# Routed mixture of experts in three chunks, with results stored by tile and gathered by token

## The chip, the cores and the metric

The kernel runs on one core of one Trainium2 chip. The metric is the device time of one execution in microseconds. It was timed three times before the change: 2657.74, 2648.60 and 2647.09 us, median 2648.6 us.

## The reference, cut to what matters

The program is a stack of ten small layers over 8 sequences of 512 tokens with 128 channels (4096 tokens): `rwkv, attn0, moe0, alibi, attn0, moe0, light, moe1, diff, moe1`. The change touches the layer `moe1` alone, which is there twice, as the eighth layer and as the tenth and last. All it computes is this (x is layer-normalised before it, and the result is added to x):

```
xt = x.reshape(-1, embed_dim)                       # 4096 tokens x 128
logits = xt @ w_gate                                # 8 experts
top_logits, sel = jax.lax.top_k(logits, 2)
probs = jax.nn.softmax(top_logits, axis=-1)
h = silu(einsum('td,edh->eth', xt, w1)) * einsum('td,edh->eth', xt, w3)    # 256 wide
y = jnp.einsum('eth,ehd->etd', h, w2)
out = einsum('ktd,tk->td', y[sel.T, t_idx[None, :], :], probs)
```

The reference computes every expert for every token; the kernel computes only the two that each token has chosen.

## The kernel before, in words

A layer `moe1` is `routed_block`. Every engine has its own instruction stream, written by hand in program order, and the streams meet at semaphores. There is no scheduler: an instruction that waits holds up all that stands behind it on its engine.

**Preparation of a sequence** (`prepare`, in 14 steps): VectorE takes the statistics (`statistics`), GpSimd the power -0.5 of the variance (`token_scale`, L5034), VectorE the shift (`shifted`, L4876), ScalarE writes the normalised rows twice, once for each chosen expert (`tokens`, L4783); TensorE turns them and computes the 8 logits (`head_turned`, `gate`), VectorE picks the two largest (`chosen`), GpSimd computes an exponential (L230), VectorE the two weights (`weighted`), TensorE and VectorE the place of each row in its expert's region (`ranks`, `placed`). Then GpSimd issues 8 indirect DMAs (`sort`, L5043), each of which scatters 128 rows of 132 numbers (the token and its weight) to the tensor `sorted` in HBM. Step k of the sequence after comes 6 turns later. The rows have two buffers, so ScalarE's `tokens(j)` waits until the rows of sequence j-2 have landed in `sorted`.

**Tiles.** When all sequences of a chunk are sorted, `tabled` (L4929 to L4955, 14 operations of VectorE) makes a table: for each tile of 128 rows its expert's weights and its address. SP then writes a padding block behind each expert's rows (`pads`, 8 DMAs, L4620 and L4621), waits for them and for the sorted rows, and loads the tiles one after the other (`tile`, L4627 and L4628) into 10 slots of `xt`. A chunk of s sequences has 8s+7 tiles. One turn of the tile loop is on TensorE the product with w1 and w3 of tile i (`up`, L4716), the product with w2 of tile i-2 (`down`, L4732), the turning of tile i+2 (L4708) and of g of tile i-1 (L4724); on ScalarE silu and two copies from PSUM; on VectorE `result(i-2)` (L4969, PSUM to y) and `product_g(i)` (L4961, called g below). Into turns 0 to 31 of chunk 0 the preparation of the second chunk's sequences is woven.

**Way back.** Each row carries its destination (column `DEST`). GpSimd scatters each finished tile by it, one indirect DMA for each tile (`result`, L5048), to the tensor `results`, which is laid out by token. y has 4 slots; VectorE, before it fills a slot again, and SP, before it loads tile n, wait for such a scatter (`result_out`). SP later loads a sequence's results, two plain DMAs of 256 KB (`results`, L4634), and VectorE adds them to x (`added`, L4975 and L4977). The four sequences of chunk 0 are added within chunk 1, the four of chunk 1 behind the last tile.

A chunk's order on the engines is fixed by `turns(c)` (its tiles plus 2); `prepare(c + 1, i)` is called in turn i. In the eighth layer the first steps of the next layer (`opening`) stand in the last chunk; four of its operations are on GpSimd.

## Time and profile before

| | us |
|---|---|
| median of 3 runs | 2648.6 |
| profiled execution | 2655.23 |
| its span | 2653.5 |
| first routed layer: its start to the first g | 1540.0 to 1611.1 |
| its chunk 0 (39 tiles), first g to last g | 1611.1 to 1725.8 |
| its chunk 1 (39 tiles), first g to last g | 1749.2 to 1813.1 |
| its last addition ends | 1832.5 |
| second routed layer: first g to the last addition's end | 2430.9 to 2650.0 |

A profile gives each instruction's start and duration and, in square brackets, how long its engine stood idle before it and what ended that. Times are microseconds from the start of the span. Only one execution is profiled, and it took 6.6 us more than the median of the timed runs.

### The profile page before, as it was taken

Reading aid. Unit: us, or ns where it says so; the run is one execution under the profiler, and the core shown is the slowest. Engines: PE = TensorE matmul, PEld = TensorE weight load, DVE = VectorE, ACT = ScalarE, POOL = GpSimd, SP = SyncE. Lnnn points to the kernel's source line nnn. Section 1 sums busy time; section 2 is a strip of 40 time slices with the busy share of each in tenths; the row PEclk is TensorE's granted clock in tenths of the full one; section 3 lists DMA queues with packets and bytes.
Section 4 is the critical chain, followed back from the end, with each engine's and each line's share of the span. In section 5 each row is a group of like instructions: output and inputs, shape, how many; then the busy total and the mean of one; then the engine's idle time right before and its main releaser. Section 6 shows DMA issues by size and latency. Waiting matters only on the chain. (4 is left out here: it accounts for less than half of the span.)

```text
span 2653.5 us, 40505 instructions
## 1 busy us (share of the span) xinstructions
PE 2185.5 (82%) x11776; PEld 1305.5 (49%) x11776; DVE 1653.2 (62%) x4436; ACT 1286.1 (48%) x2268; POOL 1425.6 (54%) x1403
## 2 busy tenths in 40 slices
PE   4577997998779989979999945776999999964666
PEld 3344564666755556644444433444444444433444
DVE  6855775776667757756666643335787787743434
ACT  4633454332435533336666623443677677643334
POOL 5923754443347533436666654645676666525644
PEclk8778898999969989989999967887999999866788
DMA  1000111222011122210000032132000000021224
...
DMA packets 106957, 112.58 MB, mean 42 GB/s; under 512 B 21816, under 2 KB 86200, under 8 KB 106488
## 3 DMA queue, kind: packets, MB, share of 16 engines
...
## 5 line engine op out<-in xcount | busy, mean ns | idle before, releaser
L2332 DVE TENSOR_REDUCE l_diffneg_max<-psum 128x1 fp32r<-128x512 f32 x512 | 335.7, 685 | 101.7 <-PE psum L2070 92.9
L2247 ACT ACTIVATE l_diffweights<-psum 128x1024 f32<-128x1024 f32 x256 | 262.0, 1026 | 141.1 <-PE psum L2099 139.9
L2070 PE MATMUL psum<-l_diffkz,l_diffQ 128*128 128x512 f32 (+1 forms) x512 | 240.0, 488 | 2.7 <-DVE l_diffneg_max L2332 1.8
L5048 POOL DMA_INDIRECT results<-l_moe1y,l_moe1xt x156 | 149.6, 959 | 156.3 <-DVE l_moe1y L4969 136.3
L2871 ACT ACTIVATE l_lightswapped<-psum 32x512 f32<-32x512 f32 x304 | 179.0, 589 | 102.0 <-DVE l_lightturned L2963 98.6
L1597 DVE TENSOR_REDUCE l_attn0neg_max<-psum 128x1 fp32r<-128x512 f32 x256 | 167.2, 683 | 51.6 <-PE psum L1328 48.9
L1503 ACT ACTIVATE l_attn0weights<-psum 128x1024 f32<-128x1024 f32 x128 | 130.4, 1023 | 115.2 <-PE psum L1350 115.2
L1724 POOL TENSOR_TENSOR l_attn0half_sums<-l_attn0weights 128x2048 f32<-128x2048 f32 x30 | 137.2, 4572 | 86.2 <-ACT l_attn0weights L1503 86.2
L4296 ACT ACTIVATE l_moe0s<-psum 128x512 f32<-128x512 f32 x144 | 85.8, 596 | 198.7 <-PE psum L855 176.0
L4716 PE MATMUL psum<-l_moe1w,l_moe1zt 128*128 x312 | 178.4, 656 | 0.0
L4732 PEld LDWEIGHTS psum<-l_moe1w,l_moe1gt 128*128 128x128 f32 x624 | 92.5, 202 | 158.8 <-issue 158.6
L175 POOL TENSOR_TENSOR settled<-powers 128x1 f32<-128x1 f32 x97 | 24.4, 251 | 257.1 <-DVE l_alibimv L702 68.9
L223 POOL TENSOR_TENSOR l_moe0ex<-powers,l_moe0hot 128x32 f32<-128x32 f32 x14 | 76.5, 5468 | 154.3 <-DVE l_moe0hot L274 154.3
L4732 PE MATMUL psum<-l_moe1w,l_moe1gt 128*128 x624 | 104.7, 293 | 64.2 <-DVE l_moe1y L4969 40.7
L4217 PE MATMUL psum<-l_moe0g,l_moe0w_raw 128*128 128x512 f32 x288 | 148.3, 600 | 7.4 <-ACT l_moe0out_sb L4271 7.4
L2070 PEld LDWEIGHTS psum<-l_diffkz,l_diffQ 128*128 128x128 f32 (+1 forms) x512 | 97.4, 190 | 115.9 <-issue 68.4
L5043 POOL DMA_INDIRECT sorted<-l_moe1rows,l_moe1row_idx x128 | 124.0, 969 | 46.7 <-issue 35.8
L2485 POOL TENSOR_TENSOR l_difflow_rows<-l_diffwhole,l_diffmarks 128x512 fp32r<-128x512 f32 x63 | 65.5, 1040 | 144.3 <-ACT l_diffwhole L2231 141.7
L2113 PE MATMUL psum<-l_diffweights,x 128*32 128x512 f32 x1024 | 141.3, 625 | 0.0
L2099 PE MATMUL psum<-l_diffQ,l_diffkz 32*128 32x512 f32 (+1 forms) x512 | 131.8, 503 | 4.6 <-issue 3.2
L4961 DVE SCALAR_TENSOR_TENSOR l_moe1g<-l_moe1s,l_moe1xt,psum 128x256 f32<-128x256 f32 x156 | 73.6, 472 | 95.5 <-ACT l_moe1s L4805 95.5
L1328 PE MATMUL psum<-l_attn0K,l_attn0Q 96*128 96x512 f32 x256 | 123.2, 518 | 7.3 <-DVE x L1619 1.7
...
## 6 DMA issues: line engine op xcount, KB each, us to landing
...
l_moe1xt<-sorted SPq DMA_DIRECT2D x156, 66.0 KB, 1.8
l_attn0Q<-l_attn0q_hi SPq DMA_DIRECT2D x128, 64.0 KB
l_moe1yb<-results SPq DMA_DIRECT2D x32, 256.0 KB, 3.3
...
```

Source lines behind the costliest of these rows:

```text
L1597: nc.vector.tensor_reduce(neg_max[:, n % 2, st, hh:hh + 1], ps[:, bank_of(("max", n, b)), :], AXX, ALU.max, negate=True).then_inc(vec_max. ...
L1724: nc.gpsimd.tensor_tensor(halves[:, a, :, :], weights[:, 2 * a, :, :], weights[:, 2 * a + 1, :, :], ALU.add).then_inc(pool_sum.sem, pool_s ...
L2070: nc.tensor.matmul(ps[:, bank, :], Q[rows, n % 4, st * P:(st + 1) * P], kz[rows, n % 4, hh, :], start=True, stop=True).then_inc(pe_max.sem ...
L2099: ins = nc.tensor.matmul(ps[:, S[m % 2] + h, :], kz[rows, n % 4, hh, tt * P:(tt + 1) * P], Q[rows, n % 4, :], start=True, stop=True)
L2113: ins = nc.tensor.matmul(ps[strip(hh), O, :], V[:, j % 2, tt, g * PER_GROUP + hh, :], weights[:, tt, hh, :], start=(tt == 0), stop=(tt == ...
L2247: nc.scalar.activation(weights[:, tt, 2 * pair:2 * pair + 2, :], ps[:, S[m % 2]:S[m % 2] + 2, :], ACT.Exp, scale=SCALE).then_inc(act_exp.s ...
L2332: nc.vector.tensor_reduce(neg_max[:, n % 2, st, row:row + 1], ps[:, bank_of(("max", n, b)), :], AXX, ALU.max, negate=True).then_inc(vec_ma ...
L2871: copy = lambda to, frm: nc.scalar.activation(to, frm, ACT.Copy)
L4217: ins = nc.tensor.matmul(ps[:, OUT, :], weights_in.raw[:, c:c + P], g[:, n % G_RING, h, :], **ends)
L4716: nc.tensor.matmul(ps[:, H[n % 2], :], zt[:, n % 2, :], w[:, bass.ds(w_at, 4 * P)], start=True, stop=True).then_inc(pe_up.sem, pe_up.step( ...
L4732: ins = nc.tensor.matmul(ps[:, Y, 0:P], gt[:, n % 2, h * P:(h + 1) * P], w[:, bass.ds(w_at + (4 + h) * P, P)], start=h == 0, stop=h == 1)
L5048: p.indirect_dma_start(core.dram["results"], bass.IndirectOffsetOnAxis(ap=xt[:, n % SLOTS, R.DEST:R.DEST + 1].bitcast(U32), axis=0), y[:, ...
```

## The change: chunks, way back and tables

Three things are changed in `routed_block`, and some constants with them.

1. The 8 sequences go in three chunks of 3, 3 and 2, which have 31, 31 and 23 tiles (85 in place of 78 per layer). The constant operations at the start shrink: the padding block is kept once, the destinations are gone.
2. Finished tiles are no longer scattered by GpSimd. SP stores them in pairs by a plain DMA, in the order of the tiles (`pair`). VectorE works out in each chunk, in turn 4, for each token the two rows at which its results lie (`way_back`, 6 operations), and GpSimd gathers them with 8 indirect DMAs of 128 rows for each sequence (`gathered`). `GATHERED` and `ADDED` say in which (chunk, turn) the gathers are issued and the additions made; sequences 6 and 7 are gathered, and 5 to 7 added, behind the last tile. SP's tile load waits for g of the tile 10 before, no longer for a scatter.
3. `tabled(c)` follows at once on the placing of the chunk's last sequence, and its addresses of the padding blocks come first in it; SP writes the padding as soon as it has loaded the chunk before.

```diff
-    SEQS = (4, 4)
+    SEQS = (3, 3, 2)
+    GATHERED = {(1, 20): 0, (1, 27): 1, (2, 0): 2, (2, 6): 3, (2, 12): 4, (2, 18): 5}
+    ADDED = {(1, 30): 0, (2, 2): 1, (2, 8): 2, (2, 16): 3, (2, 22): 4}
```

On SP:

```diff
             def tile(c, t):
                 n = R.FIRST_TILE[c] + t
-                if n >= SLOTS:
-                    result_out(sp, n - SLOTS)
+                wait(sp, vec_g, n - SLOTS, "g")
...
-            def results(j):
-                wait(sp, vec_add, j - 2, "second")
-                for k in range(2):
-                    frm = core.dram["results"][k * NSEQ * T + j * T:k * NSEQ * T + (j + 1) * T, :]
-                    sp.dma_start(yb[:, j % 2, k, :, :], frm.rearrange("(q p) d -> p q d", p=P)).then_inc(y_loaded[j % 2], 16)
+            def pair(m):
...
+                wait(sp, vec_y, n + many - 1, "y")
+                sp.dma_start(core.dram["results"][c][t * P:(t + many) * P, :].rearrange("(t p) d -> p t d", p=P), y[:, m % PAIR_SLOTS, 0:many, :]
+                             ).then_inc(y_out[m % PAIR_SLOTS], 16)
...
             for c in range(R.CHUNKS):
+                n0 = R.FIRST_TILE[c]
                 pads(c)
+                if c:
+                    m = pairs_to(m, n0 - 8)
                 for j in range(max(last_of(c) - 1, 0), last_of(c) + 1):
                     rows_sorted(sp, j)
                 sp.wait_ge(padded[c], 16 * 8)
+                wait(sp, vec_table, c, "row")
                 for t in range(R.TILES[c]):
                     tile(c, t)
+                    if n0 + t >= 12:
+                        m = pairs_to(m, n0 + t - 12)
```

On VectorE:

```diff
             def tabled(c):
...
+                inc(v.tensor_copy(table[:, c, PAD_AT:PAD_AT + 8], run[:, :]), "pads")
                 inc(v.tensor_tensor(count[:, :], run[:, :], base[:, :], ALU.subtract), "count")
...
                 if due(c, k, 9) is not None:
                     placed(due(c, k, 9))
+                    if due(c, k, 9) == last_of(c):
+                        tabled(c)
...
             def result(n):
                 vec_y.start()
                 wait(d, pe_down, n, "down")
-                if n >= YS:
-                    result_out(d, n - YS)
+                m, half = place_of(n)
+                pair_out(d, m - PAIR_SLOTS)
...
                     prepare(c + 1, i)
+                    if i == WAY_BACK:
+                        way_back(c)
+                    if (c, i) in R.ADDED:
+                        added(R.ADDED[c, i])
```

On GpSimd:

```diff
-            def result(n):
-                wait(p, vec_y, n, "y")
-                p.indirect_dma_start(core.dram["results"], bass.IndirectOffsetOnAxis(ap=xt[:, n % SLOTS, R.DEST:R.DEST + 1].bitcast(U32), axis=0),
-                                     y[:, n % YS, :], None).then_inc(y_out[n % YS], 16)
+            def gathered(j):
+                c = chunk_of(j)
+                wait(p, vec_back, c, "back_idx")
+                if j == R.FIRST[c]:
+                    last = R.FIRST_PAIR[c] + R.PAIRS[c]
+                    for m in range(last - PAIR_SLOTS, last):
+                        pair_out(p, m)
+                wait(p, vec_add, j - 2, "second")
+                for k in range(2):
+                    for q in range(NQ):
+                        p.indirect_dma_start(yb[:, j % 2, k, q, :], None, core.dram["results"][c],
+                                             bass.IndirectOffsetOnAxis(ap=back_idx[:, j, k * NQ + q:k * NQ + q + 1], axis=0)
+                                             ).then_inc(y_loaded[j % 2], 16)
```

**GpSimd in chunk 0 of the first routed layer.** In a row before (`sorted` is a sort, `results` a scatter of a finished tile, `e` the exponential; x6 means six in a row):

```order
L5034 TENSOR_TENSOR l_moe1scale<-l_moe1var,powers 128x4
L5048 DMA results<-l_moe1y,l_moe1xt 10112x128 x6
L5034 TENSOR_TENSOR l_moe1scale<-l_moe1var,powers 128x4
L230 TENSOR_TENSOR l_moe1e<-powers,l_moe1p 128x4
L5048 DMA results<-l_moe1y,l_moe1xt 10112x128 x3
L5043 DMA sorted<-l_moe1rows,l_moe1row_idx 18304x132 x2
L5048 DMA results<-l_moe1y,l_moe1xt 10112x128
```

and now:

```order
L5072 TENSOR_TENSOR l_moe1scale<-l_moe1var,powers 128x4 x2
L230 TENSOR_TENSOR l_moe1e<-powers,l_moe1p 128x4
L5081 DMA sorted<-l_moe1rows,l_moe1row_idx 14208x132 x6
L5072 TENSOR_TENSOR l_moe1scale<-l_moe1var,powers 128x4
L230 TENSOR_TENSOR l_moe1e<-powers,l_moe1p 128x4
L5081 DMA sorted<-l_moe1rows,l_moe1row_idx 14208x132 x8
```

The scatters between the sorts are gone, so scale and exponential follow one another with no finished tile between them.

**GpSimd at the end of the same layer.** Before (`open_...` are the next layer's first steps):

```order
L5043 DMA sorted<-l_moe1rows,l_moe1row_idx 18304x132 x2
L5048 DMA results<-l_moe1y,l_moe1xt 10112x128 x42
L175 TENSOR_TENSOR settled<-powers 128x1
L453 TENSOR_SCALAR open_var<-open_mv 128x4
L457 TENSOR_TENSOR open_scale<-open_var,powers 128x4
L468 TENSOR_TENSOR open_z<-x,open_mv 128x512
L470 TENSOR_TENSOR open_z<-open_z,open_scale 128x512
L5048 DMA results<-l_moe1y,l_moe1xt 10112x128 x6
```

and now (`yb<-results` is a gather):

```order
L5081 DMA sorted<-l_moe1rows,l_moe1row_idx 14208x132 x10
L5094 DMA l_moe1yb<-results,l_moe1back_idx 128x128 x24
L175 TENSOR_TENSOR settled<-powers 128x1
L453 TENSOR_SCALAR open_var<-open_mv 128x4
L457 TENSOR_TENSOR open_scale<-open_var,powers 128x4
L468 TENSOR_TENSOR open_z<-x,open_mv 128x512
L470 TENSOR_TENSOR open_z<-open_z,open_scale 128x512
L5094 DMA l_moe1yb<-results,l_moe1back_idx 128x128 x40
```

Of the 64 gathers, 24 stand ahead of the next layer's steps and 40 behind them, the last 16 of which need the last tile's store.

**VectorE between two chunks.** Before, the table of chunk 1 stood behind the last two tiles' results (`y`), ahead of the next chunk's first two g:

```order
L4961 SCALAR_TENSOR_TENSOR l_moe1g<-l_moe1s,l_moe1xt,psum 128x256
L4969 COPY l_moe1y<-psum 128x128 x2
L4929 TENSOR_TENSOR l_moe1count<-l_moe1run,l_moe1base 128x8
L4931 TENSOR_SCALAR l_moe1whole<-l_moe1count 128x8
L4933 TENSOR_SCALAR l_moe1tiles_i<-l_moe1whole 128x8
```

and now it follows on `placed` of the last sequence, in turn 21 of chunk 0:

```order
L4937 TENSOR_REDUCE l_moe1row_at<-l_moe1picked 128x8
L4939 CAST l_moe1row_idx<-l_moe1row_at 128x8
L4940 TENSOR_TENSOR l_moe1run<-l_moe1run,psum 128x8
L4947 CAST l_moe1table<-l_moe1run 128x8
L4948 TENSOR_TENSOR l_moe1count<-l_moe1run,l_moe1base 128x8
L4950 TENSOR_SCALAR l_moe1whole<-l_moe1count 128x8
```

The 14 operations have moved from the gap between the chunks into the tile loop.

## Rows read from the trace of the kernel before

**Rows 1.** The page: span; busy us, share and instructions of each engine.

```profile
span 2653.5 us, 40505 instructions
...
PE 2185.5 (82%) x11776; PEld 1305.5 (49%) x11776; DVE 1653.2 (62%) x4436; ACT 1286.1 (48%) x2268; POOL 1425.6 (54%) x1403
```

**Rows 2.** Busy time by stretch: start:end, length, five engines, TensorE's clock, DMA share, GB/s.

```profile
core 0: us, PE busy (x) PEld busy (x) DVE busy (x) ACT busy (x) POOL busy (x), PEclk, DMA share, GB/s
1611.10:1726.30 115.20, 85.48 (x416) 57.17 (x414) 48.72 (x257) 50.98 (x149) 72.51 (x75) 0.86 0.20 59
1726.30:1749.20 22.90, 4.79 (x16) 2.86 (x17) 3.77 (x16) 1.32 (x5) 4.03 (x5) 0.57 0.18 52
1749.20:1813.60 64.40, 62.71 (x340) 41.64 (x338) 32.12 (x94) 38.22 (x119) 37.06 (x40) 0.99 0.36 105
1813.60:1832.50 18.90, 1.63 (x10) 1.21 (x10) 7.19 (x15) 0.38 (x1) 3.83 (x4) 0.62 0.44 128
2430.90:2545.30 114.40, 84.35 (x416) 57.07 (x414) 48.33 (x257) 50.77 (x149) 72.54 (x75) 0.86 0.20 60
2568.20:2630.80 62.60, 62.06 (x336) 41.11 (x334) 30.92 (x84) 37.05 (x113) 34.56 (x37) 0.99 0.44 127
```

**Rows 3.** Instructions by time, GpSimd, first routed layer's start (start, length, what, idle).

```profile
1577.84 0.96 POOL L5043 DMA_INDIRECT sorted<-l_moe1rows,l_moe1row_idx  x1 [0.97 <-DVE l_moe1run L4922]
...
1590.84 0.96 POOL L5043 DMA_INDIRECT sorted<-l_moe1rows,l_moe1row_idx  x1 [0.91 <-DVE l_moe1run L4922]
...
1599.67 0.96 POOL L5043 DMA_INDIRECT sorted<-l_moe1rows,l_moe1row_idx  x1 [0.30 <-issue]
```

**Rows 4.** The same stretch: the padding block's clearing, SP's pads and first tile loads.

```profile
1542.27 1.67 DVE L4850 MEMSET l_moe1spare<- 128x1935 f32 x1 [0.35 <-issue]
...
1594.87 8.50 SPq L4621 DMA_DIRECT2D sorted<-l_moe1spare  x8
1605.43 14.77 SPq L4628 DMA_DIRECT2D l_moe1xt<-sorted  x12
```

**Rows 5.** Chunk 0 by time: g of tiles 6 and 12, two waits of the preparation.

```profile
1623.97 0.47 DVE L4961 SCALAR_TENSOR_TENSOR l_moe1g<-l_moe1s,l_moe1xt,psum 128x256 f32<-128x256 f32 x1
...
1631.09 0.16 DVE L4876 SCALAR_TENSOR_TENSOR l_moe1shift<-l_moe1mv,l_moe1scale 128x4 f32<-128x4 f32 x1 [1.95 <-POOL l_moe1scale L5034]
...
1641.45 0.47 DVE L4961 SCALAR_TENSOR_TENSOR l_moe1g<-l_moe1s,l_moe1xt,psum 128x256 f32<-128x256 f32 x1
...
1656.36 3.18 ACT L4783 ACTIVATE l_moe1rows<-x,l_moe1shift,l_moe1scale 128x128 f32<-128x128 f32 x8 [8.55 <-DMA sorted<-l_moe1rows,l_moe1row_idx]
```

**Rows 6.** Between the chunks: table's first operation, SP's pads, first turned tile.

```profile
1728.80 0.16 DVE L4929 TENSOR_TENSOR l_moe1count<-l_moe1run,l_moe1base 128x8 f32<-128x8 f32 x1
...
1733.09 8.32 SPq L4621 DMA_DIRECT2D sorted<-l_moe1spare  x8
...
1745.30 0.48 PE L4708 MATMUL psum<-ident,l_moe1xt 128*128 128x128 f32 x1 [16.74 <-DMA l_moe1xt<-sorted]
```

**Rows 7.** DMA issues: count, KB of each, median us from issue to landing.

```profile
sorted<-l_moe1spare SPq DMA_DIRECT2D x32, 66.0 KB, 1.6
...
sorted<-l_moe1rows,l_moe1row_idx POOLq DMA_INDIRECT x128, 2.3
out<-x SPq DMA_DIRECT2D x8, 256.0 KB, 2.5
```

**Rows 8.** GpSimd's first and last operation for the next layer.

```profile
1807.04 0.21 POOL L175 TENSOR_TENSOR settled<-powers 128x1 f32<-128x1 f32 x1
...
1809.79 1.04 POOL L470 TENSOR_TENSOR open_z<-open_z,open_scale 128x512 f32<-128x512 f32 x1
```

**Rows 9.** Second layer: a scatter beside an addition, and the last addition.

```profile
2617.64 0.96 POOL L5048 DMA_INDIRECT results<-l_moe1y,l_moe1xt  x1 [0.68 <-DVE l_moe1y L4969]
...
2617.67 0.70 DVE L4975 TENSOR_TENSOR x<-x,l_moe1yb 128x512 f32<-128x512 f32 x1
...
2649.28 0.69 DVE L4977 TENSOR_TENSOR x<-x,l_moe1yb 128x512 f32<-128x512 f32 x1
```

More of the change, by code:

```diff
@@ L4518 @@
     WIDTH = P + 4
-    WEIGHT, DEST = P, P + 1
-    SPARE = 2 * NSEQ * T
+    WEIGHT = P
     COLS = 6 * P
+    PAIRS = [(many + 1) // 2 for many in TILES]
+    FIRST_PAIR = [0, *accumulate(PAIRS)][:CHUNKS]
+    GATHERED = {(1, 20): 0, (1, 27): 1, (2, 0): 2, (2, 6): 3, (2, 12): 4, (2, 18): 5}
+    ADDED = {(1, 30): 0, (2, 2): 1, (2, 8): 2, (2, 16): 3, (2, 22): 4}
+    OPENED = 2
     @staticmethod
@@ L4599, in rows_sorted, with place_of, pair_out @@
             engine.wait_ge(sorted_out[j % 2], 16 * 2 * NQ * (j // 2 + 1))
-        def result_out(engine, n):
-            engine.wait_ge(y_out[n % YS], 16 * (n // YS + 1))
+        def place_of(n):
+            c = max(c for c in range(R.CHUNKS) if R.FIRST_TILE[c] <= n)
+            pair, half = divmod(n - R.FIRST_TILE[c], 2)
+            return R.FIRST_PAIR[c] + pair, half
+        def pair_out(engine, m):
+            if m >= 0:
+                engine.wait_ge(y_out[m % PAIR_SLOTS], 16 * (m // PAIR_SLOTS + 1))
         @block.sync
@@ L4748, in _ @@
                 expert_of = lambda i: t.value_load(table[0:1, c, W_AT + i:W_AT + i + 1], min_val=0, max_val=7 * R.COLS)
-                wait(t, vec_table, c, "pads")
+                wait(t, vec_table, c, "row")
                 at_w = {0: expert_of(0)}
@@ L4954, in tabled, with way_back @@
                 inc(v.tensor_scalar(table[:, c, ROW_AT:ROW_AT + many], at_row[:, 0:many], float(8 * R.REGION + R.SPARES - 1), float(P), ALU.min, ALU.mult), "row")
-                inc(v.tensor_copy(table[:, c, PAD_AT:PAD_AT + 8], run[:, :]), "pads")
+            def way_back(c):
+                vec_back.start()
+                inc = lambda ins, key: ins.then_inc(vec_back.sem, vec_back.step(key))
+                wait_for = lambda key: d.wait_ge(vec_back.sem, vec_back.done(c, key))
+                many = R.SEQS[c] * 2 * NQ
+                mine = slice(R.FIRST[c], R.FIRST[c] + R.SEQS[c])
+                inc(v.tensor_tensor(first_tile[:, :], ends[:, :], tiles[:, :], ALU.subtract), "first_tile")
+                wait_for("first_tile")
+                inc(v.scalar_tensor_tensor(offset[:, :], first_tile[:, :], float(P), base[:, :], ALU.mult, ALU.subtract), "offset")
+                wait_for("offset")
+                inc(v.tensor_tensor(moved[:, 0:many, :], hots[:, mine, :, :].rearrange("p j k e -> p (j k) e"),
+                                    offset[:, :].unsqueeze(1).to_broadcast([P, many, 8]), ALU.mult), "moved")
+                wait_for("moved")
+                inc(v.reduce_sum(shifts[:, 0:many], moved[:, 0:many, :], AXX), "shifts")
+                wait_for("shifts")
+                inc(v.tensor_tensor(back[:, 0:many], shifts[:, 0:many], row_at[:, mine, :].rearrange("p j k -> p (j k)"), ALU.add), "back")
+                wait_for("back")
+                inc(v.tensor_copy(back_idx[:, mine, :].rearrange("p j k -> p (j k)"), back[:, 0:many]), "back_idx")
             def product_g(n):
@@ L5013, in _ @@
                     prepare(c + 1, k)
-            for j in range(R.FIRST[-1], NSEQ):
+            for j in range(len(R.ADDED), NSEQ):
                 added(j)
@@ L5063, in _ @@
             for c in range(R.CHUNKS):
-                n0 = R.FIRST_TILE[c]
                 for i in turns(c):
-                    if 0 <= i - 2 < R.TILES[c]:
-                        result(n0 + i - 2)
                     prepare(c + 1, i)
-                    if opening and c == R.CHUNKS - 1 and i == COMBINE + 2 + BETWEEN * R.SEQS[c - 1]:
-                        opening.scale(p)
-                        opening.tokens(p)
+                    if (c, i) in R.GATHERED:
+                        gathered(R.GATHERED[c, i])
+                        if opening and R.GATHERED[c, i] == R.OPENED:
+                            opening.scale(p)
+                            opening.tokens(p)
                 for k in spare_turns(c):
                     prepare(c + 1, k)
+            for j in range(len(R.GATHERED), NSEQ):
+                gathered(j)
 def product3(nc, out, x_hi, x_lo, w_hi, w_lo):
```

99 lines of the change are left out of this document (48 added, 51 removed).

## The prediction

> **What bounds the kernel now.** I read the busy time by stretch first, for the two routed layers alone, since nothing else is touched. The page shows a GpSimd that is busy 54% of the whole span [rows 1], which says nothing of these layers; the stretches do. In the first routed layer the tile loop of chunk 0 takes 114.7 us from the first g to the last (the stretch of 115.2 us less one g of 0.5), or 3.0 us for a tile; chunk 1, with as many tiles, takes 63.9 us; the second layer's chunk 1 takes 62.1 us, or 62.1 / 38 = 1.63 us for a tile, which I take as the loop's own pace [rows 2]. In chunk 1 TensorE is busy 62.7 of 64.4 us, in chunk 0 85 of 115 [rows 2]. So chunk 0 pays 114.7 - 38 x 1.63 = 52.7 us beyond the pace. Its four preparations cost part of that. The rest is GpSimd: it issues one indirect DMA every (1599.67 - 1590.84) / 7 = 1.26 us [rows 3], and its 75 instructions there [rows 2] are 67 DMAs (35 scatters, 32 sorts), 84.5 us at that pace, and 8 powers and exponentials of about 1 us each (72.5 busy us less 67 x 0.96); what it holds back is to be seen as VectorE's 1.95 us wait for a scale that stood behind a finished tile, and as ScalarE's 8.55 us wait for sorted rows that had not landed [rows 5].
>
> Between the chunks lie 1749.2 - 1725.8 = 23.4 us. The table starts only at 1728.80, SP's padding at 1733.09 takes 8.3 us, and the first tile is turned at 1745.30 [rows 6]. TensorE does 4.8 us of work in that stretch [rows 2]. Ahead of chunk 0 there is 71 us of preparation, in which each sequence costs 1590.84 - 1577.84 = 13.0 us [rows 3]. Behind chunk 1 there are 18.9 + 0.5 us of loads and additions [rows 2]. From the first g to the end of the last addition it is 221.4 us in the first layer and 2649.97 - 2430.9 = 219.1 us in the second [rows 2, 9].
>
> **Before chunk 0.** One sequence less is prepared: -13.0 us. The rest by what is late: the last sort is issued at 1599.67 and lands 2.3 us later, 1602.0 [rows 3, 7]; the padding is issued from 1594.87 to 1603.4 and lands 1.6 us after its last issue, and with the address's load the first tile is issued at 1605.43 [rows 4, 7]. With the pads' addresses first in the table, SP begins some 3.7 us earlier, so that the sorts become the last: with about 0.8 us for the address the tile goes out at 1602.8, -2.6 us. Clearing 7 blocks in place of 15 takes 0.8 us in place of 1.67 [rows 4]: -0.9. Sum -16.5 us in each layer. The lower bound is -13; for more than -16.5 a sequence would have to cost more than it does.
>
> **The tile loops.** 85 tiles in three chunks have 82 intervals in place of 76. A preparation without GpSimd's queue: the six turns from tile 6 to 12 hold one whole preparation, and took 1641.45 - 1623.97 = 17.5 us, 7.7 over the pace; the wait of 1.95 us for the scale lies in it [rows 5], and with scatters gone it goes. I take 5.5 us for each sequence, between 4 and 7.7.
> The table in the loop (14 operations, 1728.80 to about 1732.3, 3.5 us) finds some room in a turn, as VectorE is busy 30.9 / 38 = 0.8 of 1.63 us in the second layer's chunk 1 [rows 2], and some in the next: +2.3 us for each of two chunks, at most 3.5. The way back (6 small operations, estimated 1.5 us from the table's) fits beside the loop like an addition (2 x 0.7 us [rows 9]; the second layer's chunk 1 held four of them at 1.63 us a tile): 0, at most 1.5.
> Chunk 0, 31 tiles: 30 x 1.63 = 49.0, 3 preparations 16.5, table 2.3, TensorE's clock at the start 0.6 (an estimate; the granted clock was 0.86 over chunk 0 and 0.99 over chunk 1 [rows 2]), and tokens(5), which waits for the rows of sequence 3 (8 x 1.26 + 2.3 us plus scale and exponential of about 1 us each, against 5 turns that hold half a preparation) 1.5: 69.9 us. Chunk 1: 49.0 + 11.0 + 2.3 = 62.3, and 0.5 for the next layer's statistics in the first layer.
>
> **Between the chunks.** The pads are issued from turn 20 or 21 of the chunk before, last 8.3 us, and land 2 us later, in about turn 27; chunk 1's last sorts land 12.4 us after turn 21. So the tiles are there, and a boundary costs the drain and refill: 1728.8 - 1725.8 = 3.0, 1749.2 - 1745.3 = 3.9 and a little for the expert's address, 7.0 us in place of 23.4 [rows 2, 6], but twice.
>
> **From the last g of chunk 1 (time 0).** SP loads the next tiles at about the pads' pace, 8.32 / 8 = 1.04 us each [rows 6], with pair stores of an estimated 0.4 between them; the last pair of chunk 1 stands behind the 12th load, which waits for g of the second tile at 8.6 us. Issued at 10.1, landed at 12.1 (128 KB: between the 1.6 us of 66 KB and the 2.5 of 256 KB [rows 7]). GpSimd then issues the gathers of sequences 2 to 5, 32 x 1.26 = 40.4 us, to 52.5. The addition of 2, in turn 8 at 7 + 13 = 20 us, finds its rows landed only at 12.1 + 8.8 + 2.3 + 1.3 = 24.5: the loop stands 4.5 us. The last y is there at 7 + 22 x 1.63 + 4.5 + 2.8 = 50.2 us, its pair has landed at 52.6. Then 16 gathers: the last is issued 15 x 1.26 later, at 71.7, lands at 74.0, and the addition (1.4) ends at 75.5 us. In the first layer the next layer's four steps (1807.04 to 1810.8, 3.8 us [rows 8]) stand in GpSimd's queue: 79.3 us.
>
> **Sum.** First layer: 69.9 + 7.0 + 62.8 + 79.3 = 219.0 against 221.4. Second: 69.9 + 7.0 + 62.3 + 75.5 = 214.7 against 219.1. To this I add 4 us a layer for waits that such a sum misses (two handoffs at each of the boundaries, y's slots and SP's queue, each between 0 and the 1.95 us of [rows 5]; I take 1): 223.0 and 218.7. So the loops give back nearly nothing, and the gain is the start: -16.5 + 1.6 and -16.5 - 0.4, together -31.8 us. Profiled execution 2655.2 - 31.8 = 2623.4; the median lies 6.6 us lower than the profiled execution, so 2617 us.
>
> What the sum rests on and no row shows is the issue of a gather; the only row is that of the scatters, 1.26 us. Below it, at best, lies the 0.96 us of the instruction itself [rows 3]: 48 of them stand on the path of each layer, so -29 us for both. Upward I take 1.6 us as the bound of the range, +33 us.
>
> **A rule of the Trainium skill.** A scatter beside an addition, whose operands both lie in SBUF, took 0.96 us like every other [rows 9]. The page "SBUF — State Buffer", section "Who interferes with whom", says that a VectorE instruction with two SBUF inputs and a GpSimd instruction that reads SBUF block each other for the whole of the one that came first. The trace does not bear this out for scatters. If it came true for gathers, as a mechanism of this kernel: five additions of 2 x 0.7 us in each layer would hold GpSimd's chain, +7 us a layer, 2631 us in all.
>
> **The rivals.**
> 1. *The loops lose their waits more fully than I credit.* No missed handoffs (-8) and 4 us a preparation (-15 for ten): 2594 us; for it speaks that GpSimd has only 24 sorts in 31 turns.
> 2. *Chunk 0 stays coupled.* Sorts, scale, exponential and ScalarE's wait for landed rows also hold without scatters; chunk 0's 3.0 us a tile would make 90.6 us of it, +20.7 a layer, 2658 us, no change; half of it 2638. For it speaks the 8.55 us wait, which is for sorts [rows 5]; against it that in that stretch half of GpSimd's issues were scatters.
> 3. *The gathers become the bound, and it is slower than before.* Place: GpSimd from chunk 1's last store to the end. Each 0.1 us on a gather costs 48 x 0.1 x 2 = 9.6 us. From 1.60 us an issue the gain is gone, from 1.73 it is slower by over 0.5%; at 1.9 it would be 2678 us. For it: the gathers stand alone on the path at the end; against it: both directions describe 128 rows.
> 4. *SP comes late at the boundaries* (pads not ahead of the chunk's end): each boundary keeps its 23.4 us, +16.4 x 4, 2683 us. Against it: the pads need the placing of turn 21 (15 in chunk 1) alone.
> 5. *The port lock*, above: 2631 us.
>
> **How the numbers follow.** Forecast 0.60; rival 1 0.08; rival 2 0.14; rival 3 0.08; rival 4 0.05; rival 5 0.05. What a measurement of this kernel can tell from no change is about 0.5%, 13 us: faster is below 2635. The forecast, rival 1, rival 5 mostly (0.04) and a part of rival 2 (0.03) are faster: 0.75. The rest of rival 2 (0.11), 0.01 of rival 3, 0.02 of rival 4 and 0.01 of rival 5 are no change: 0.15. Slower is 0.10. Range 2598 to 2642: downward cheaper gathers and preparations, upward half of rival 2 and a gather of 1.5 us; the forecast's own range is 2603 to 2633.
>
> **What the new profile would show.** The first tile load of the first routed layer at about 1590 (the start); g of chunk 0 over about 70 us, with VectorE's wait for the scale short; 7 us from the last g of a chunk to the next g, twice; gathers at 1.26 us an issue, one after the other from about 12 us behind the last g of chunk 1 to the layer's end; one wait of VectorE of some 4 us ahead of the addition of sequence 2; 29 us (before 19.4) from the last g to the last addition. Wrong would be: chunk 0 over 80 us (rival 2), gathers over 1.5 us apart (3), pads behind the last y (4).

## The result, and the profile after

The changed kernel took 2616.95 us (median of 4 runs, 2610.84 to 2622.14) against 2653.17 us (median of 4, 2647.09 to 2657.81): a ratio of 0.9876, 95% interval 0.9849 to 0.9904. It is faster by 1.2%, and the forecast of 2617 us was met. That it was met to the microsecond is luck: the forecast was 2623.4 us for the profiled execution, which took 2619.28, and a median 6.6 us below it, where it lies 2.3 us below. How far the steps of the forecast were met is answered further down.

The page of the changed kernel, span and busy time:

```profile
span 2617.1 us, 41303 instructions
...
PE 2194.2 (84%) x11902; PEld 1310.5 (50%) x11902; DVE 1669.7 (64%) x4510; ACT 1297.8 (50%) x2310; POOL 1398.6 (53%) x1371
```

The busy time by stretch answers to [rows 2] (start:end, length, five engines, TensorE's granted clock as a share of 2.4 GHz, DMA share, GB/s). In order: chunk 0, the boundary, chunk 1, the boundary, chunk 2 and the way back of the first routed layer; then chunk 2 of the second.

```profile
core 0: us, PE busy (x) PEld busy (x) DVE busy (x) ACT busy (x) POOL busy (x), PEclk, DMA share, GB/s
1596.00:1673.90 77.90, 63.21 (x324) 43.30 (x322) 40.55 (x213) 39.00 (x115) 29.57 (x30) 0.91 0.28 76
1673.90:1680.10 6.20, 4.25 (x16) 2.52 (x17) 1.05 (x4) 1.73 (x6) 0.00 (x0) 0.87 0.33 89
1680.10:1742.40 62.30, 55.48 (x304) 37.07 (x302) 34.90 (x168) 35.34 (x106) 31.06 (x33) 0.99 0.35 94
1742.40:1750.60 8.20, 4.83 (x17) 2.87 (x17) 3.58 (x15) 1.74 (x6) 6.37 (x7) 0.76 0.52 137
1750.60:1788.30 37.70, 37.51 (x196) 24.54 (x194) 19.93 (x55) 22.07 (x69) 29.33 (x33) 0.96 0.41 114
1788.30:1819.00 30.70, 2.15 (x10) 1.62 (x10) 7.57 (x17) 0.77 (x2) 17.73 (x19) 0.55 0.17 49
...
2548.30:2584.20 35.90, 35.82 (x192) 23.40 (x190) 19.38 (x56) 20.80 (x65) 26.30 (x28) 0.99 0.51 139
```

GpSimd in chunk 0 is down from 75 instructions and 72.5 us to 30 and 29.6. The boundary of 22.9 us in [rows 2] has become one of 6.2 and one of 8.2. The last stretch, 18.9 us before, is 30.7 now, and in it GpSimd is the only engine with much to do.

SP in that layer answers to [rows 4, 6] (SPq: from the first issue to the last):

```profile
1578.81 8.63 SPq L4634 DMA_DIRECT2D sorted<-l_moe1spare  x8
1590.36 14.80 SPq L4640 DMA_DIRECT2D l_moe1xt<-sorted  x14
...
1655.72 8.43 SPq L4634 DMA_DIRECT2D sorted<-l_moe1spare  x8
...
1668.05 7.03 SPq L4640 DMA_DIRECT2D l_moe1xt<-sorted  x7
```

The pads of chunk 1 begin 18 us before the last g of chunk 0 (at 1673.90), and its first tile is requested 5.9 us before that g. GpSimd's gathers, the first of sequence 2 and those around the end of chunk 2:

```profile
1747.32 0.94 POOL L5094 DMA_INDIRECT l_moe1yb<-results,l_moe1back_idx  x1 [0.30 <-issue]
...
1787.98 0.94 POOL L5094 DMA_INDIRECT l_moe1yb<-results,l_moe1back_idx  x1 [0.30 <-issue]
1789.23 0.98 POOL L5094 DMA_INDIRECT l_moe1yb<-results,l_moe1back_idx  x1 [0.30 <-issue]
1790.52 0.94 POOL L5094 DMA_INDIRECT l_moe1yb<-results,l_moe1back_idx  x1 [0.30 <-issue]
1795.73 0.94 POOL L5094 DMA_INDIRECT l_moe1yb<-results,l_moe1back_idx  x1 [4.27 <-DMA results<-l_moe1y]
...
1815.16 0.94 POOL L5094 DMA_INDIRECT l_moe1yb<-results,l_moe1back_idx  x1 [0.30 <-issue]
```

and VectorE's additions beside and behind them, as [rows 9]:

```profile
1788.71 0.68 DVE L5012 TENSOR_TENSOR x<-x,l_moe1yb 128x512 f32<-128x512 f32 x1
...
1793.03 0.29 DVE L5006 COPY l_moe1y<-psum 128x128 f32<-128x128 f32 x1 [1.50 <-PE psum L4752]
...
1817.60 0.69 DVE L5012 TENSOR_TENSOR x<-x,l_moe1yb 128x512 f32<-128x512 f32 x1 [8.55 <-DMA l_moe1yb<-results,l_moe1back_idx]
1818.33 0.69 DVE L5014 TENSOR_TENSOR x<-x,l_moe1yb 128x512 f32<-128x512 f32 x1
```

The last y is copied at 1793.03, its pair is stored, and the first gather that needs it starts at 1795.73. The start of the sixteenth follows 19.4 us later; most are 1.25 us apart, the second 1.87. VectorE goes on 2.4 us after the last one's start, and its addition ends the layer at 1819.0. The issue of a gather costs what that of a scatter did.

The kernels side by side, in us, read from each trace as first routed layer / second; the four runs that come first below are not in the table. "Lead" runs from the layer's first VectorE instruction on the ranks' constants to the first g, a chunk from its first g to its last, a "gap" from there to the next g, "tail" from the last g to the last addition's end.

| kernel | ratio, 95% | lead | chunk 0 | gap | chunk 1 | gap | chunk 2 | tail | layer |
|---|---|---|---|---|---|---|---|---|---|
| before | 1 | 69.8/68.7 | 114.7/113.9 | 23.4/23.4 | 63.9/62.1 | | | 19.4/19.7 | 291.2/287.8 |
| changed | 0.9876 | 53.1/52.9 | 77.9/74.8 | 6.2/5.5 | 62.3/63.2 | 8.2/6.7 | 37.7/35.9 | 30.7/29.0 | 276.1/267.9 |
| early_again | 0.9894, 0.9857-0.993 | 67.2/66.7 | 115.9/115.1 | 9.4/7.7 | 64.4/62.2 | | | 19.8/20.1 | 276.7/271.8 |
| two_again | 0.9937, 0.9899-0.9975 | 65.9/65.9 | 96.9/101.2 | 5.9/5.5 | 64.5/62.1 | | | 48.5/48.4 | 281.6/283.1 |
| late_again | 1.001, 0.9969-1.0052 | 53.1/53.1 | 72.4/71.4 | 20.4/19.9 | 59.1/59.0 | 22.7/20.0 | 38.0/37.0 | 30.6/29.3 | 296.5/289.6 |
| rows3 | 0.9784, 0.9753-0.9814 | 51.1/50.2 | 68.3/70.1 | 5.5/6.2 | 63.1/62.0 | 8.1/6.4 | 38.1/36.4 | 30.1/28.9 | 264.2/260.2 |
| before_rows3 | 0.992, 0.9891-0.995 | 66.3/65.7 | 107.4/108.1 | 24.2/23.5 | 65.1/62.5 | | | 19.3/20.1 | 282.2/279.9 |
| early_rows3 | 0.9802, 0.9767-0.9836 | 64.2/63.8 | 111.0/112.5 | 6.1/5.5 | 63.5/61.8 | | | 19.5/20.3 | 264.3/263.8 |
| no_last_gathers | 0.9755, 0.9721-0.9788 | 53.3/53.0 | 76.8/73.2 | 5.5/5.5 | 61.6/61.6 | 8.1/6.6 | 38.0/36.3 | 21.6/20.4 | 264.9/256.5 |
| chunks_233 | 0.9976, 0.9953-0.9998 | 38.3/38.1 | 61.4/59.8 | 15.1/15.2 | 73.0/72.5 | 9.7/10.2 | 54.2/51.3 | 38.5/38.3 | 290.2/285.5 |

Of the 36.3 us between the two spans, 15.1 lie in the first routed layer and 19.9 in the second, 3.4 in the layer between them, which the change does not touch; against this, the stretch ahead of the first is 1.6 longer and the one behind the last addition 0.5. That untouched layer took between 517.8 and 530.2 us over the kernels of the table, so single traces are compared here by segments of the routed layers, and kernels by their ratios.

The four experiments that come first below ran in a set of executions in which the kernel before took 2706.49 us and the engines stood still inside the routed layers for nothing that the profile names; three of them were run again later ("again" in a name means that), `scatter_three` was not.

### The profile page after: what moved, and what is told of

It is laid out like the page before. It is cut to its first block and busy times, and to the rows that moved or that the text cites. A ratio compares the mean times of both kernels' runs of the same rounds, so it can differ in the third digit from the quotient of the medians.

```text
span 2617.1 us, 41303 instructions
## 1 busy us (share of the span) xinstructions
PE 2194.2 (84%) x11902; PEld 1310.5 (50%) x11902; DVE 1669.7 (64%) x4510; ACT 1297.8 (50%) x2310; POOL 1398.6 (53%) x1371
## 5 line engine op out<-in xcount | busy, mean ns | idle before, releaser
L2871 ACT ACTIVATE l_lightswapped<-psum 32x512 f32<-32x512 f32 x304 | 178.7, 588 | 100.6 <-DVE l_lightturned L2963 97.2
L1597 DVE TENSOR_REDUCE l_attn0neg_max<-psum 128x1 fp32r<-128x512 f32 x256 | 167.2, 683 | 50.6 <-PE psum L1328 47.8
L4736 PE MATMUL psum<-l_moe1w,l_moe1zt 128*128 x340 | 189.2, 640 | 0.0
L1724 POOL TENSOR_TENSOR l_attn0half_sums<-l_attn0weights 128x2048 f32<-128x2048 f32 x30 | 137.2, 4572 | 87.5 <-ACT l_attn0weights L1503 87.5
L4752 PEld LDWEIGHTS psum<-l_moe1w,l_moe1gt 128*128 128x128 f32 x680 | 98.3, 197 | 150.0 <-issue 150.0
L175 POOL TENSOR_TENSOR settled<-powers 128x1 f32<-128x1 f32 x97 | 24.2, 249 | 258.4 <-DVE l_alibimv L702 69.7
L4752 PE MATMUL psum<-l_moe1w,l_moe1gt 128*128 x680 | 112.4, 290 | 52.1 <-ACT l_moe1gt L4831 27.1
L2070 PEld LDWEIGHTS psum<-l_diffkz,l_diffQ 128*128 128x128 f32 (+1 forms) x512 | 97.0, 189 | 114.4 <-issue 66.7
L5094 POOL DMA_INDIRECT l_moe1yb<-results,l_moe1back_idx x128 | 122.6, 958 | 48.2 <-issue 39.4
L4371 DVE TENSOR_TENSOR l_moe0sc<-l_moe0s,l_moe0bcs 128x512 f32<-128x512 f32 x128 | 93.5, 730 | 56.0 <-ACT l_moe0s L4296 51.9
```

The costliest lines, as they stand in the source:

```text
L1597: nc.vector.tensor_reduce(neg_max[:, n % 2, st, hh:hh + 1], ps[:, bank_of(("max", n, b)), :], AXX, ALU.max, negate=True).then_inc(vec_max. ...
L1724: nc.gpsimd.tensor_tensor(halves[:, a, :, :], weights[:, 2 * a, :, :], weights[:, 2 * a + 1, :, :], ALU.add).then_inc(pool_sum.sem, pool_s ...
L2070: nc.tensor.matmul(ps[:, bank, :], Q[rows, n % 4, st * P:(st + 1) * P], kz[rows, n % 4, hh, :], start=True, stop=True).then_inc(pe_max.sem ...
L2871: copy = lambda to, frm: nc.scalar.activation(to, frm, ACT.Copy)
L4736: nc.tensor.matmul(ps[:, H[n % 2], :], zt[:, n % 2, :], w[:, bass.ds(w_at, 4 * P)], start=True, stop=True).then_inc(pe_up.sem, pe_up.step( ...
L4752: ins = nc.tensor.matmul(ps[:, Y, 0:P], gt[:, n % 2, h * P:(h + 1) * P], w[:, bass.ds(w_at + (4 + h) * P, P)], start=h == 0, stop=h == 1)
```

## The experiments

**1. Which of the three edits brings the gain?** Two chunks with gathers and early tables; the kernel before with early tables alone; the kernel before in three chunks; the changed kernel with late tables.

```diff
 two_chunks: the changed kernel with
-    SEQS = (3, 3, 2)
+    SEQS = (4, 4)
+    GATHERED = {(1, 0): 0, (1, 6): 1, (1, 12): 2, (1, 18): 3}
+    ADDED = {(1, 12): 0, (1, 19): 1, (1, 26): 2, (1, 33): 3}
 early_only: the kernel before with
+                    if due(c, k, 9) == last_of(c):
+                        tabled(c)
-                tabled(c)
 scatter_three: the kernel before with
-    SEQS = (4, 4)
+    SEQS = (3, 3, 2)
 late_tables: the changed kernel with
-                    if due(c, k, 9) == last_of(c):
-                        tabled(c)
+                tabled(c)
```

Each diff shows the edit's main lines. In `early_only` the pads' addresses also come first in the table, and the waits on the table follow that; in `late_tables` SP also writes the pads behind the pair stores; in `scatter_three` the turns in which finished sequences are added, and the next layer's steps on GpSimd, are moved to fit the shorter chunks.

> The changed kernel (stores by tile, gathers by token, early tables) with two chunks of 4 and 4 sequences as before the change. My accounting: against the kernel before, each layer's start is 3.5 us shorter (pads early, smaller clearing), chunk 0 takes 38 x 1.63 + 4 preparations of 5 + table 2.5 + two waits of 5.7 for landed rows = 97 in place of 114.7 us, the boundary 7 in place of 23.4, but behind the last tile stand 32 gathers of 1.25 us in place of plain loads, some 49 in place of 19.4 us. Sum -8 to -9 us a layer: about 2636 us. Rival (the chunks' number gives nothing, the way back and the tables give it all): as the changed kernel, about 2617 us.

Measured: 2733.94 us, ratio 1.0122 (1.007 to 1.0174). Chunk 1 took 94.8 / 97.3 us.

> The kernel before with the early tables alone: two chunks, scatters by tile on GpSimd. My accounting: start -2.6 us, table in the loop +2.4, boundary 7 to 9 in place of 23.4 us; sum about -15 us a layer, 2622 us. Rival (GpSimd's queue of scatters and sorts runs late at the chunk's end, so that SP's tile loads, which wait for scatters, still come late): half of it or less, 2638 us or more.

Measured: 2664.23 us, ratio 0.9854 (0.9817 to 0.9891); gaps 6.2 / 5.5, but chunk 0 139.1 / 137.2 us.

> The kernel before with chunks of 3, 3 and 2 sequences alone: scatters by tile on GpSimd, late tables. My accounting: start -13 us, but two boundaries of 23.4 us in place of one, 7 tiles more and 7 scatters more on a GpSimd that holds the loops back: +29 us a layer, about 2710 us. Rival (a smaller first chunk alone brings the gain): 13 us a layer less, 2627 us.

Measured: 2757.25 us, ratio 1.0204 (1.0164 to 1.0245); lead 56.8 / 55.9, gaps of 22.6 to 23.1 us in both places, tail 14.8 / 13.9. As expected in lead and gaps, which hold no loop: a third chunk with late tables buys 13 us of lead with one more gap of 23. The tail, 4.6 to 5.8 us shorter, was not in the expectation.

> The changed kernel with each table made at the start of its chunk, as before the change (SP stores the pairs first and then writes the padding). My accounting: start +2.6 us, -2.4 us for each of two tables in the loops, two boundaries of 23.4 in place of 6 to 7 us: +31 us a layer, about 2678 us. Rival (SP's loads and the drain hide most of the table): at most +10 us, 2627 us.

Measured: 2808.86 us, ratio 1.0375 (1.0345 to 1.0404); gaps 19.7 to 23.5, but chunk 1 97.0 / 97.2 and chunk 2 61.9 / 61.8.

In absolute time all four lie 42 to 131 us above what was expected. Against the kernel before, itself 53 us slower in this set, `early_only` and `scatter_three` come out near it (0.9854 for an expected 0.988, 1.0204 for 1.021), `two_chunks` and `late_tables` do not (1.0122 for 0.994, 1.0375 for 1.009). The excess lies in the loops. TensorE's longest waits in chunk 1 of `two_chunks` (in total, times, longest) name no cause:

```profile
PE psum L4752 <- issue: 19.7, 4, 9.3
PE psum L4752 <- ACT l_moe1gt L4831: 9.3, 4, 4.9
```

In `late_tables` VectorE lost 27.5 us there in two waits, again without a releaser in the kernel:

```profile
DVE l_moe1y L5006 <- remote: 27.5, 2, 18.3
```

In the traces outside this set no such wait of VectorE or TensorE inside the loops is longer than 1.0 us. That made two theories, the kernels or the execution, and the same kernels were run again.

> The same kernel as two_chunks, run again. Theory A: in that run every engine stood for up to 10 us at a time for nothing that the profile names (TensorE 42 us ahead of the down product, VectorE 24 us ahead of y), the kernel before it too had 2706 us in place of 2653; in the kernels of the second set no such row is over 1.1 us. So these waits are a condition of that execution and not of the order of the instructions. Then this run has no idle time of over 2 us without a releaser in the routed layers, chunk 1 takes 64 to 68 us in place of 95, the tail stays 49 us, and the ratio is 0.99 to 1.00 (the 2636 us first expected would be 0.994). Theory B: eight sequences gathered in two chunks do make chunk 1 wait (the gathers of four sequences in a row, y's slots behind them): chunk 1 takes 90 us or more again, ratio 1.01 again.

Measured: 2639.85 us, ratio 0.9937. Chunk 1 64.5 / 62.1, tail 48.5 / 48.4. Its TensorE waits in the same window:

```profile
PE psum L4752 <- DVE l_moe1y L5006: 1.7, 2, 1.0
PE psum L4752 <- ACT l_moe1gt L4831: 1.7, 3, 0.6
```

> The same kernel as early_only, run again (two chunks, scatters, two row buffers, tables early). Theory A: 2653 - 2 x (17.4 of the boundary) + 2 x 3 (tables in the loop) - 2 x 2.6 (pads early) = 2620 us, ratio 0.988; chunk 0 near 116 us in place of the 139 of the disturbed run. Theory B, the 139 us belong to the early table in chunk 0: ratio stays 0.985 by the same disturbance of both, or chunk 0 is 135 us or more here and the ratio is over 1.

Measured: 2630.57 us, ratio 0.9894; gaps 9.4 / 7.7, chunk 0 115.9 / 115.1.

> The same kernel as late_tables, run again (three chunks, gathers, tables at the chunk's start). Theory A, the stalls of 10 to 19 us inside chunks 1 and 2 were that execution's: boundaries 20 to 23 us again (+15 each, four of them, +60), the start 0 to +2.6 each, chunks 1 and 2 at 62 and 37 us: 2617 + 61 = 2678 us, ratio 1.009. Theory B, with late pads SP runs behind in the chunk and y's slots and g wait for it: chunk 1 97 and chunk 2 62 us again, ratio 1.037.

Measured: 2662.32 us, ratio 1.001 (0.9969 to 1.0052); gaps 19.9 to 22.7; chunk 1 59.1 / 59.0, chunk 2 38.0 / 37.0. The loops are as Theory A has them, but its 1.009 lies above the interval: it added the gaps and did not take off what the tables had cost inside the loops, 16.3 us by the table's rows. VectorE in chunk 1:

```profile
DVE l_moe1g L4998 <- ACT l_moe1s L4825: 17.6, 3, 14.2
DVE l_moe1y L5006 <- PE psum L4752: 17.6, 19, 1.8
...
DVE l_moe1y L5006 <- issue: 1.3, 2, 1.0
```

Theory A (the execution) held three times. A ratio to the kernel before, taken in the same set, did not take the disturbance out: 1.0122 became 0.9937, 1.0375 became 1.001, and 0.9854 became 0.9894. What was at first expected of the segments stood nearly everywhere once it was gone. The later runs were on another chip, but this alone does not explain it: on the first chip the kernel before took 2654.24 us in the next set. What disturbed that set was not settled.

Read together: early tables alone are -1.1%; gathering, in two chunks and with early tables, is no gain over that (0.9937 against 0.9894: chunk 0 is 14 to 19 us shorter, the tail 28 longer); three chunks and gathering without early tables are no gain at all (1.001). All three make 0.9876 (0.9849 to 0.9904), not to be told from early tables alone (0.9857 to 0.993), and measured in another set than these three.

**2. Is ScalarE's wait for landed rows what is left of chunk 0's coupling?** A third buffer for the rows that are sorted, in the changed kernel and in the one before.

```diff
-        rows = sb("rows", [P, 2, 2, NQ, R.WIDTH])
+        rows = sb("rows", [P, 3, 2, NQ, R.WIDTH])
...
-                if j >= 2:
-                    rows_sorted(a, j - 2)
+                if j >= 3:
+                    rows_sorted(a, j - 3)
```

The row numbers and the semaphores of the sorts become three as well, and SP waits for three sequences.

> The changed kernel with three buffers for the rows that are sorted (and their indices) in place of two, so that ScalarE's tokens(j) waits for the sorts of sequence j-3. Theory (chunk 0 stands because tokens(5) waits 5.7 us for the rows of sequence 3): chunk 0 shorter by 4 to 6 us in each layer, 2607 us. Rival (the stall only moves to VectorE's wait for the scale, which stands behind six sorts on GpSimd): 0 to -2 us, 2616 us.

Measured: 2596.76 us (5 rounds), ratio 0.9784 (0.9753 to 0.9814). In the changed kernel GpSimd's sorts of sequence 3 and ScalarE's rows of sequence 5 stand so:

```profile
1620.18 1.03 POOL L5081 DMA_INDIRECT sorted<-l_moe1rows,l_moe1row_idx  x1 [7.25 <-DVE l_moe1run L4940]
...
1631.11 0.96 POOL L5081 DMA_INDIRECT sorted<-l_moe1rows,l_moe1row_idx  x1 [0.30 <-issue]
1640.44 0.96 POOL L5081 DMA_INDIRECT sorted<-l_moe1rows,l_moe1row_idx  x1 [8.37 <-DVE l_moe1run L4940]
```

```profile
1628.74 0.38 ACT L4831 ACTIVATE l_moe1gt<-psum 128x256 f32<-128x256 f32 x1
1634.81 3.18 ACT L4803 ACTIVATE l_moe1rows<-x,l_moe1shift,l_moe1scale 128x128 f32<-128x128 f32 x8 [5.69 <-DMA sorted<-l_moe1rows,l_moe1row_idx]
```

The last sort of sequence 3 starts at 1631.11, ScalarE goes on 3.7 us later, at 1634.81, and GpSimd, whose sorts it waited for, then waits itself 8.37 us for VectorE: a circle. With three buffers ScalarE does not stop:

```profile
1629.57 0.38 ACT L4831 ACTIVATE l_moe1gt<-psum 128x256 f32<-128x256 f32 x1
1629.85 3.17 ACT L4803 ACTIVATE l_moe1rows<-x,l_moe1shift,l_moe1scale 128x128 f32<-128x128 f32 x8
```

Chunk 0 falls by 9.6 / 4.7 us and the lead by 2.0 / 2.7, where 4 to 6 us were expected in chunk 0. Of the 9.6 us, 5.8 are the interval between two g that held the wait, 2.5 the two intervals behind it, and 1.4 three intervals behind the table. TensorE's clock shows where the 2.5 come from. In the changed kernel the stretch behind it, and the one behind that:

```profile
1640.00:1645.00 5.00, 5.00 (x19) 3.60 (x17) 1.54 (x5) 2.28 (x6) 3.65 (x4) 0.57 0.34 96
1645.00:1648.00 3.00, 3.00 (x21) 2.36 (x20) 1.91 (x12) 1.01 (x4) 2.10 (x3) 1.00 0.39 111
```

For 5 us TensorE has work all the time at a granted clock of 0.57, mostly the lower of its two levels, 1.2 GHz, after 6 us in which it did 1.2 us of work; with three buffers it stays at 1.00. The Trainium skill, "TensorE: Matmul & The Clock Gate", section "What's actually happening", says that the default is the throttled state and that activity releases it; the trace agrees with this, 0.57 and then 1.00.

> The kernel before with three buffers for the rows. Theory (GpSimd's issue of 67 DMAs is not by itself the bound of chunk 0, it is coupled to ScalarE's two waits of 8 us for landed rows): chunk 0 shorter by some 8 us a layer, about 2637 us. Rival (GpSimd's issue is the bound, any other wait is filled up by it): no change, 2653 us.

Measured: 2632.43 us (5 rounds), ratio 0.992. The kernel before has such waits too (8.55 us in [rows 5]), and the edit takes 7.3 / 5.9 us out of chunk 0 and 3.5 / 3.0 out of the lead.

**3. Do the two small edits alone do as much as the whole?** Both in the kernel before.

> The kernel before with early tables and a third buffer of sorted rows, nothing else: two chunks, results scattered. If the two gains add, 0.988 x 0.992 = 0.980, 2600 us, within 5 us of the changed kernel with three row buffers (2597): then three chunks and gathering bring nothing of their own over the two small edits. If three chunks and gathering are what made room, it stays at 2615 or more.

Measured: 2606.13 us, ratio 0.9802 (0.9767 to 0.9836), where the product of the two expected ratios was 0.980. The changed kernel with three buffers has 0.9784 (0.9753 to 0.9814), in another set of executions: the intervals overlap, and by segments the layers take 264.3 / 263.8 us here and 264.2 / 260.2 there. So over these two edits three chunks and gathering have shown at most a few us by segments (0 and 3.5); the two ratios leave room for a gain of up to some 17 us.

**4. Is the tail the gathers?** The gathers of the last sequence are left out, so its addition adds what the buffer held.

```diff
-                d.wait_ge(y_loaded[j % 2], 16 * 2 * NQ * (j // 2 + 1))
+                if j < NSEQ - 1:
+                    d.wait_ge(y_loaded[j % 2], 16 * 2 * NQ * (j // 2 + 1))
...
-                for k in range(2):
+                for k in range(2 if j < NSEQ - 1 else 0):
```

> The changed kernel without the 8 gathers of sequence 7 (its additions are made with what stands in the buffer). Theory (the last 16 gathers of each layer stand on the path one by one): 8 x 1.25 = 10 us a layer less, about 2597 us. Rival (the path at the end is the pair's store, the landing and the additions): -2 us a layer, 2613 us.

Measured: 2591.68 us, ratio 0.9755; tail 21.6 / 20.4, or 9.1 / 8.6 less. VectorE's last wait and addition:

```profile
1808.90 0.69 DVE L5013 TENSOR_TENSOR x<-x,l_moe1yb 128x512 f32<-128x512 f32 x1 [11.70 <-DMA l_moe1yb<-results,l_moe1back_idx]
...
1810.95 0.69 DVE L5015 TENSOR_TENSOR x<-x,l_moe1yb 128x512 f32<-128x512 f32 x1
```

Eight gathers at 1.25 us are 10.0; the addition that they no longer hide, 1.4 us, now follows the other. What is left, 8.6 us, is the measured 9.1 / 8.6: a gather of the last sequence costs the tail its full spacing.

**5. Is a shorter first chunk better still?**

```diff
-    SEQS = (3, 3, 2)
+    SEQS = (2, 3, 3)
+    GATHERED = {(1, 26): 0, (1, 27): 1, (2, 0): 2, (2, 6): 3, (2, 12): 4}
+    ADDED = {(2, 2): 0, (2, 8): 1, (2, 14): 2, (2, 20): 3, (2, 26): 4}
```

SP's pads go behind the pair stores of the chunk before in it.

> The changed kernel with chunks of 2, 3 and 3 sequences (23, 31 and 31 tiles), with its gathers and additions in the turns that this leaves, and SP storing pairs ahead of the padding. My accounting: start -13 us, one preparation more in the loops +5, the first boundary later by some 7 us (the last sorts of chunk 1 land when chunk 0 has ended), 8 gathers more behind the last tile +10: +9 us a layer, 2635 us. Rival (each sequence taken from the start is worth its 13 us): 2591 us.

Measured: 2646.86 us, ratio 0.9976. The lead falls by 14.8, but the first gap is 15 us (the last sequence is placed in turn 21 of 23, so the pads begin 2.6 us before the last g), chunk 1 holds three preparations and the coupling again (an interval of 6.8 us between two g), and the tail has 8 gathers more (+7.8 / +9.3). A layer is 14.1 / 17.6 us longer than in the changed kernel, where 9 were expected: the sum of such terms was right in sign and too small. What the lead gives, the first gap and the end take.

## Why the forecast was right, and which steps were not

| us, first / second layer | forecast | measured |
|---|---|---|
| lead | -16.5 | -16.7 / -15.8 |
| chunk 0 | 69.9 | 77.9 / 74.8 |
| first gap | 7.0 | 6.2 / 5.5 |
| chunk 1 | 62.8 / 62.3 | 62.3 / 63.2 |
| from its last g to the end | 79.3 / 75.5 | 76.6 / 71.6 |
| waits that no row names | 4 / 4 | none found |
| from the first g to the end | 223.0 / 218.7 | 223.0 / 215.0 |

**Right.** The lead, by its parts: one preparation less is -13.0 / -12.8 (`scatter_three`), the pads' addresses first in the table -2.6 / -2.0 (`early_again`), both and the smaller clearing -16.7 / -15.8. The first tile load at 1590.36, forecast "about 1590". The gaps: early tables cut them by 13 to 14.5 us each in three chunks. A preparation without scatters: chunk 1 of `late_again` holds two of them, no table and no wait for landed rows, and its 59.1 / 59.0 less 49.0 for the tiles are 5.0 us for each, where I took 5.5. The gathers at 1.25 us, forecast 1.26; tail 30.7 / 29.0, forecast 29. That the loops give back nearly nothing and the start is the gain held in the first layer (223.0 against 221.4) and less in the second (215.0 against 219.1).

**Wrong: tokens(5).** I took 1.5 us for its wait; the row says 5.69. The 1.5 does not even follow from its own figures: 14.4 us of sorts, scale and exponential less 5 turns (8.2) and half a preparation (2.75) are 3.5. And the trace leaves only the 8.9 us from 1620.18 to the end of ScalarE's last work at 1629.12 of the 14.6 us to 1634.81, and the rest is the wait. That TensorE's clock falls behind it, another 2.5 us, was no term at all. This was half of rival 2 in small: sorts alone do couple, as [rows 5] said, to 5.7 and not to 20.7 us. `rows3` shows it as a cause: without it chunk 0 is 68.3 / 70.1, against 68.4 in my sum without the 1.5. That this is so near is partly luck, since the table costs more than I took and a preparation less.

**Wrong: the table in the loop.** I took 2.3 us and at most 3.5. Against `late_again` it costs 5.5 / 3.4 in chunk 0 and 3.2 / 4.2 in chunk 1. VectorE from the table's first operation to the next y, which stands ahead of the next g (chunk 0):

```profile
1654.80 0.17 DVE L4947 CAST l_moe1table<-l_moe1run 128x8 int32<-128x8 f32 x1
...
1657.98 0.18 DVE L4973 TENSOR_SCALAR l_moe1table<-l_moe1at_row 128x31 int32<-128x31 f32 x1
1658.08 0.28 DVE L5006 COPY l_moe1y<-psum 128x128 f32<-128x128 f32 x1
```

TensorE beside it (the product with w1 and w3, L4736, takes 1.02 us, then 1.92, then 1.02 again):

```profile
1654.89 1.02 PE L4736 MATMUL psum<-l_moe1w,l_moe1zt 128*128 x2
1658.61 1.22 PE L4752 MATMUL psum<-l_moe1w,l_moe1gt 128*128 x4 [2.69 <-DVE l_moe1y L5006]
...
1660.25 1.92 PE L4736 MATMUL psum<-l_moe1w,l_moe1zt 128*128 x2
...
1665.76 1.02 PE L4736 MATMUL psum<-l_moe1w,l_moe1zt 128*128 x2
```

and the stretches' clock:

```profile
1653.00:1658.00 5.00, 2.91 (x15) 1.56 (x13) 4.43 (x22) 2.04 (x7) 2.16 (x2) 1.00 0.23 64
1658.00:1661.50 3.50, 2.90 (x9) 2.33 (x10) 1.42 (x5) 0.66 (x2) 2.64 (x3) 0.50 0.36 112
1661.50:1665.00 3.50, 3.50 (x11) 2.17 (x10) 0.68 (x2) 1.04 (x3) 2.59 (x4) 0.53 0.36 110
1665.00:1670.00 5.00, 5.00 (x30) 3.43 (x28) 2.04 (x6) 2.96 (x9) 0.51 (x1) 1.00 0.39 114
```

The table delays the next turn by 3.3 us (an interval of 4.9 in place of 1.6), no part of it hidden, since 14 operations in one turn leave no room in it; and behind the idle time TensorE's clock is down for 7 us, two intervals of 3.2 and 2.6 us, 2.5 more. In chunk 1 of the first layer TensorE stands 2.25 us behind a table, its clock stays up, and the cost is the first part alone. This second part differs between executions of the same instructions: in `no_last_gathers` the table intervals are 4.9, 4.6, 4.9 and 4.6 us as here, and only one is followed by a slow one (2.6 us). Splitting the table over several turns was not tried.

**Wrong: the wait ahead of sequence 2, and GpSimd's queue at the end.** I had GpSimd gather sequences 2 to 5 in a row from the landing of chunk 1's last pair. Sequence 2 belongs to chunk 0 (chunks of 3 begin at 0, 3 and 6): its gathers ran from 1747.32 and waited for nothing in chunk 1, and the 4.5 us stall did not come. In the second layer the last y is there at 45.6 us after chunk 1's last g, the forecast 50.2 less this stall. In the first it is there at 50.6, which looks like a hit and is luck: the boundary and chunk 2 took 45.9 us where 7.0 and 22 x 1.63 make 42.9, and the last y came 4.7 us behind the last g in place of 2.8. With sequence 2 out of the way GpSimd's queue was done early: it stood 4.27 us for the last pair, so the next layer's four steps, 3.8 us in my sum of the first layer, cost nothing. Of the 48 gathers that the forecast put on the path of a layer, the trace shows only the last 16 there.

**The compensation.** In the first layer chunk 0 cost 8.0 more than forecast: 4.2 and 2.5 by the wait for rows and the clock behind it, 3.2 by the table, less some 2 for three cheaper preparations. 4.0 of it was in the sum as waits that I could not name, 0.8 and 0.5 came off the gap and chunk 1, and 2.7 off the end. That 223.0 equals 223.0 is luck; in the second layer the same terms leave 3.7. The whole gain by spans is 36.3 us where 31.8 were forecast: 3.2 of the difference are the two layers, and 1.3 lie in no step of mine, 3.4 of the untouched layer less 1.6 ahead and 0.5 behind.

**Rivals.** 1 (no lost handoffs, preparations of 4 us): its first half was there, the 4 us for handoffs were not to be found as waits; a preparation took 5.0. 2: its mechanism was there at a quarter of its price. 3: refuted, 1.25 us. 4: refuted, pads at 1655.72. 5, the lock between VectorE and GpSimd: not as forecast, but not nothing. An addition with two SBUF inputs at 1788.71 lies beside gathers of 0.94 us at 1787.98 and 0.98 at 1789.23. Over the whole trace 25 of the 128 gathers overlap an addition; 17 of them keep 0.94 to 0.96 us, eight take 0.98 to 1.45, and of the other 103 none takes over 1.07. The excess is 1.6 us in all, against 14 in the forecast of this rival; that the additions cause it is not shown, since other VectorE work stands beside the longest too. Eight scatters of the kernel before beside an addition keep 0.95 to 0.96. The rule that the prediction took from "SBUF — State Buffer" in the Trainium skill, section "Who interferes with whom", an exclusive lock for a whole instruction, was not borne out for indirect DMAs in either direction; the section itself infers that such an addition takes only the shared read interface and the making of descriptors needs the write interface, and the scatters agree with that.
